# A mixture-of-experts entry on TensorE in another order: all sums of squares behind the first projection, roots on ScalarE, and projections, transposes and router logits ahead of most expert groups

## The reference, cut to what matters

```python
def rms_norm(x):
    eps = jnp.asarray(jnp.finfo(x.dtype).eps, x.dtype)
    return x * jax.lax.rsqrt(jnp.mean(x * x, axis=-1, keepdims=True) + eps)
...
y = jnp.einsum('bhqk,bkhd->bqhd', probs, vr).reshape(bsz, seqlen, dim)
return ternary_linear(rms_norm(y), w_proj)
...
h = h + _L0_attn_ref(_layernorm(h, axis=-1), ...)
h = h + _L0_ffn_ref(_layernorm(h, axis=-1), ...)

def _L0_ffn_ref(hidden_states, gate_w, shared_gate, shared_up, shared_down, r_gate, r_up, r_down):
    x = hidden_states.reshape(-1, h)
    shared_out = _swiglu(x, shared_gate, shared_up, shared_down)
    logits = x @ gate_w.T
    top_id = jnp.argmax(logits, axis=-1)
    score = jax.nn.sigmoid(jnp.max(logits, axis=-1))
    xs = x * score[:, None]
    # routed_out: each token's xs through the SwiGLU of its expert top_id (8 experts)
    return (shared_out + routed_out).reshape(b, s, h)
```

## Time and profile before

| | |
|---|---|
| median of three runs | 574.7 us |
| the profiled execution's own time | 579.41 us |
| its span, first to last instruction | 577.6 us |
| TensorE busy | 419.8 us, 73% |
| VectorE busy | 324.2 us, 56% |
| ScalarE busy | 246.2 us, 43% |
| GpSimd busy | 143.9 us, 25% |
| mean granted TensorE clock | 0.832 |

### The profile page before, as it was taken

How to read it: one execution, slowest core, us unless ns; L and a number is a source line. 1 busy time by engine, 2 the same in 40 slices (tenths; PEclk the granted TensorE clock), 3 DMA queues, 4 the chain that set the end, 5 groups by cost and what they waited for, 6 DMA issues and landing times.

```text
span 577.6 us, 8904 instructions
## 1 busy us (share of the span) xinstructions
PE 419.8 (73%) x3189; PEld 306.6 (53%) x3189; DVE 324.2 (56%) x876; ACT 246.2 (43%) x512; POOL 143.9 (25%) x169
## 2 busy tenths in 40 slices
PE   3677884477779979999889993362497114699997
PEld 3545652256568965666555782221243013489996
DVE  3858875489653410232411116868898995645642
ACT  4235444256634411222212211396099476286661
POOL 3544433089721150000000053800000000213410
PEclk9969887569997997999999998685555555599999
DMA  8921111293003332111101071000000000000002
GB/s 278 406 99 17 20 17 14 82 425 167 2 1 146 111 109 83 36 56 37 49 25 43 23 291 37 0 1 3 1 1 0 1 2 2 1 1 0 1 19 68
DMA packets 19789, 38.59 MB, mean 67 GB/s; under 512 B 2136, under 2 KB 16164, under 8 KB 18340
## 3 DMA queue, kind: packets, MB, share of 16 engines
q1 hardware_dynamic: 18788, 35.41, 17.7%
q0 software_dynamic: 960, 2.62, 1.3%
HBM read 29.77 MB, written 7.01 MB: 64 GB/s over the span
## 4 chain that ended last, share of the span: by engine, by line
PE 46%; DVE 28%; issue 11%; ACT 8%; POOL 5%; DMA 2%; SPq 1%; DVEq 0%; ACTq 0%
PE psum L1253 11%; PE psum L1285 5%; PE psum L2334 4%; PE psum L2367 3%; PE psum L1260 3%; POOL ring L782 2%; PE psum L1299 2%; PE psum L610 2%; PE psum L2373 2%; ACT experts L1662 1%; POOL experts L787 1%; PE psum L921 1%; PE psum L1277 1%; DMA experts<-in_tern 1%; PE psum L2351 1%
## 5 line engine op out<-in xcount | busy, mean ns | idle before, releaser
L1253 PE MATMUL psum<-experts,ring 128*128 x136 | 67.1, 619 | 1.6 <-issue 1.2
L1084 DVE TENSOR_TENSOR ring<-ring,psum 128x512 f32<-128x512 f32 x17 | 11.7, 688 | 67.9 <-PE psum L1253 67.9
L1184 POOL DMA_INDIRECT front<-expert_results,slot_of x10 | 9.5, 953 | 126.4 <-DMA expert_results<-ring 123.7
L1260 PE MATMUL psum<-front,shared 128*128 128x256 f32 (+1 forms) x160 | 36.8, 383 | 0.0
L1253 PEld LDWEIGHTS psum<-experts,ring 128*128 128x128 f32 x136 | 24.4, 199 | 21.0 <-issue 20.9
L1260 PEld LDWEIGHTS psum<-front,shared 128*128 128x128 f32 x160 | 30.3, 197 | 3.5
L1285 PE MATMUL psum<-experts,ring 128*128 x136 | 32.1, 379 | 0.0
L1285 PEld LDWEIGHTS psum<-experts,ring 128*128 128x128 f32 x136 | 25.8, 190 | 10.3 <-issue 7.7
L1382 ACT COPY ring<-psum 128x512 f32<-128x512 f32 x17 | 10.0, 586 | 42.3 <-PE psum L1277 42.3
L2334 PE MATMUL psum<-experts 128*128 128x256 f32 (+1 forms) x120 | 27.4, 371 | 0.0
L590 PE MATMUL psum<-experts,ring 128*128 128x256 f32 x108 | 26.1, 393 | 0.8 <-DVE experts L485 0.7
(11 more groups left out here) (361 smaller groups left out, 1085.7 us busy)
## 6 DMA issues: line engine op xcount, KB each, us to landing
experts<-in_experts SPq DMA_DIRECT2D x8, 1536.0 KB, 12.5
experts<-in_x SPq DMA_DIRECT2D x9, 384.0 KB, 8.3
expert_rows<-zeros SPq DMA_DIRECT2D x1, 2176.0 KB, 14.8
ring<-expert_rows SPq DMA_DIRECT2D x17, 128.0 KB, 2.2
shared<-in_shared SPq DMA_DIRECT2D x1, 1536.0 KB, 18.0
experts<-in_ffn_q SPq DMA_DIRECT2D x1, 1536.0 KB
experts<-in_ffn_s SPq DMA_DIRECT2D x1, 1536.0 KB
experts<-in_pos_embed SPq DMA_DIRECT2D x1, 1152.0 KB, 9.6
```

The lines of the kernel that those rows point to most:

```text
L1084: nc.vector.tensor_tensor(o, o, up_bank(g), ALU.mult).then_inc(hidden_done.sem, 1)
L1253: mm = nc.tensor.matmul(bank, sl_xT[t % 2][:, k, :], slot_w(t, block, k, F), start=(k == 0), stop=(k == KD - 1))
L1260: mm = nc.tensor.matmul(o[:, b, 0:w], shared_w(block, k, (2 * half + b) * P, P), moe_x(c)[:, k, 0:w], start=(k == 0), stop=(k == KD - 1))
```

## The change

```diff
@@ out_scalar
             for c in range(NCH):
                 nc.scalar.activation(out_sq[...], yT[...], ACT.Square).then_inc(y_squared.sem, 1)
+            for part in range(2):
+                act.wait_ge(ms_summed.sem, ms_summed.done(part))
+                r = MS_PARTS[part]
+                nc.scalar.activation(out_ms[:, r[0]:r[-1] + 1], psum[:, 1 + part, 0:len(r)], ACT.Sqrt, bias=out_eps[:, :], scale=1.0 / D).then_inc(ms_ready.sem, 1)
@@ out_tensor
             out_projection(pe, 0)
-            summed(0)
-            summed(1)
+            for t in range(NT):
+                summed(t)
             out_projection(pe, 1)
-            for t in range(2, 6):
-                summed(t)
             out_projection(pe, 2)
-            for t in range(6, NT):
-                summed(t)
-            out_projection(pe, 3)
@@ out_vector
-            def mean(part):
-                dve.wait_ge(ms_summed.sem, ms_summed.done(part))
+            def inverted(part):
+                dve.wait_ge(ms_ready.sem, ms_ready.done(part))
                 r = MS_PARTS[part]
-                nc.vector.tensor_scalar(out_ms[...], psum[...], 1.0 / D, F32_EPS, ALU.mult, ALU.add).then_inc(ms_ready.sem, 1)
+                nc.vector.reciprocal(out_rs[...], out_ms[...]).then_inc(rs_ready.sem, 1)
...
-            joined(0)
-            joined(1)
-            mean(0)
-            for c in range(2, NCH):
+            nc.vector.memset(out_eps[:, :], F32_EPS)
+            for c in range(NCH):
                 joined(c)
+            inverted(0)
             for c in range(NCH):
                 added(c)
-                if c == 0:
-                    mean(1)
-                else:
+                if c >= 1:
                     shifted(c - 1)
                 counted(c)
+                if c == 0:
+                    inverted(1)
             shifted(NCH - 1)
@@ out_pool
-            for part in range(2):
-                pool.wait_ge(ms_ready.sem, ms_ready.done(part))
-                r = MS_PARTS[part]
-                nc.gpsimd.tensor_tensor(out_rs[...], out_ms[...], minus_half[...], ALU.pow).then_inc(rs_ready.sem, 1)
@@ moe_vector
             hidden(0)
+            chosen_experts()
             hidden(1)
-            chosen_experts()
+            routed()
             for g in range(2, GROUPS + 1):
...
-                if g == 2:
-                    routed()
@@ moe_tensor
             turned(0)
+            out_projection(pe, 3)
             logits(0)
+            turned(1)
+            out_projection(pe, NCH - 1)
+            logits(1)
+            turned(2)
             pe.wait_ge(l_shared.sem, l_shared.all)
...
                 if g == 0:
-                    turned(1)
-                    out_projection(pe, NCH - 1)
-                if g == 1:
                     logits(2)
                     turned(3)
-                if g == 2:
-                    logits(4)
                 if g < GROUPS:
                     one_of(g, 1, up_bank(g), up_done)
                 if g == 0:
-                    logits(1)
-                    turned(2)
-                if g == 1:
                     logits(3)
                     turned(4)
+                    logits(4)
+                if g == 1:
+                    rank_tokens()
@@ moe_scalar
             out_normalised(act, 1)
+            columns(1)
+            out_normalised(act, 2)
+            columns(2)
             for g in range(GROUPS + 1):
...
                 if g == 0:
-                    columns(1)
-                    out_normalised(act, 2)
-                    columns(2)
                     out_normalised(act, 3)
-                if g == 1:
                     columns(3)
                     out_normalised(act, 4)
                     columns(4)
+                    score()
+                if g == 1:
+                    scaled(range(0, NT // 2))
                 if g == 2:
-                    score()
-                    scaled(range(0, NT // 2))
-                if g == 3:
                     scaled(range(NT // 2, NT))
```

More of the change, by code:

```diff
@@ L897, in tower @@
         out_shift = sb("out_shift", [P, NT])
+        out_eps = sb("out_eps", [P, 1])
         y_squared, ms_summed, ms_ready, rs_ready = Count("y_squared"), Count("ms_summed"), Count("ms_ready"), Count("rs_ready")
@@ L949, in joined @@
                 nc.vector.tensor_tensor(out_sq[:, 0, w], out_sq[:, 0, w], out_sq[:, 1, w], ALU.add).then_inc(sq_joined.sem, 1)
-            def mean(part):
-                dve.wait_ge(ms_summed.sem, ms_summed.done(part))
+            def inverted(part):
+                dve.wait_ge(ms_ready.sem, ms_ready.done(part))
                 r = MS_PARTS[part]
-                nc.vector.tensor_scalar(out_ms[:, r[0]:r[-1] + 1], psum[:, 1 + part, 0:len(r)], 1.0 / D, F32_EPS, ALU.mult, ALU.add).then_inc(ms_ready.sem, 1)
+                nc.vector.reciprocal(out_rs[:, r[0]:r[-1] + 1], out_ms[:, r[0]:r[-1] + 1]).then_inc(rs_ready.sem, 1)
             def added(c):
@@ L979, in out_vector @@
                 nc.vector.memset(upto[u][:, :, :], 0.0)
-            joined(0)
-            joined(1)
-            mean(0)
-            for c in range(2, NCH):
+            nc.vector.memset(out_eps[:, :], F32_EPS)
+            for c in range(NCH):
                 joined(c)
+            inverted(0)
             for c in range(NCH):
                 added(c)
-                if c == 0:
-                    mean(1)
-                else:
+                if c >= 1:
                     shifted(c - 1)
                 counted(c)
+                if c == 0:
+                    inverted(1)
             shifted(NCH - 1)
         def out_pool(pool):
-            for part in range(2):
-                pool.wait_ge(ms_ready.sem, ms_ready.done(part))
-                r = MS_PARTS[part]
-                nc.gpsimd.tensor_tensor(out_rs[:, r[0]:r[-1] + 1], out_ms[:, r[0]:r[-1] + 1], minus_half[:, 0:len(r)], ALU.pow).then_inc(rs_ready.sem, 1)
             for c in range(NCH):
@@ L1300, in shared_down @@
                                               start=(k == 0), stop=(k == KF - 1))
-                    if c == 0 and u == 0:
-                        rank_tokens()
                 mm.then_inc(sh_down.sem, 1)
```

## The result

The changed kernel took 567.73 us (median of four runs, 566.22 to 569.21) against 575.4 us before (four runs): the ratio is 0.9865, interval 0.9842 to 0.9889, or 7.7 us less (6.4 to 9.1). Forecast were 564.9 us and 9.8 us less, with a range of 562.0 to 570.5; 0.7 us of the difference from 564.9 is that the kernel before took 575.4 here and 574.7 when the forecast was made. The profiled execution took 566.22 us, its span 564.1.

What follows compares the result with a forecast made beforehand. TensorE's own work was taken as the bound: 50.66 us at full clock plus 4.2 of idle made 54.9 instead of 64.66, saving 9.8 us, for a median of 564.9 us; range 562.0 to 570.5.

Steps and rivals of the forecast that it cites:

- rival A: Entry: half clock once, price 3.2 us, saving 6.6, 568.1 us, chance 0.20; twice or ahead of slots, 571.3, chance 0.05.
- the stretch: TensorE from the first projection's start to the end of the slot's first gate and up products, 64.66 us before.
- What bounds the stretch: First projection to first slot products: TensorE's own work bounds it, 50.66 us at full clock; the other 14.00 can move.
- No half clock in the stretch, as no idle is over 1.2: First projection to first slot products: full clock throughout, since 1.59 us of idle had left it full elsewhere.
- the 6.50 us of half clock: Loss behind the entry's idle and the idle ahead of the slots, together 6.50 us, claimed to go.
- The slots' share of the half clock: First slot's gate and up products: 6.52 us where one takes 1.72 at full clock, so 3.08 lost.
- The root on ScalarE: Entry: roots on ScalarE replace GpSimd's powers, 1.65 us for eight columns, at the price of a 1.28 us table load.
- rival C: Entry: a 1.4 us pause behind ScalarE's table load delays both roots; saving 8.4, 566.3 us, chance 0.05.
- Rival D: From 166 to 190 us: thinner work leaves the clock at half throughout; slower, 577.9 us, chance 0.04.
- Rival B: Ahead of the slots: scatters still set their start if `slot_of` is late; 4 us late saves 4.2, 570.5 us, chance 0.06.
- The carry to the end: Behind the first slot products: everything hangs on the slots, so the 9.8 us saving reaches the end whole.

Runs made afterwards that it cites:

- the run with 1.4 us of delay: Changed kernel with five idle VectorE operations ahead of the one that writes `slot_of`; ratio 0.9854 against the kernel before.
- the one with 4.1: Changed kernel with fifteen idle VectorE operations ahead of the one that writes `slot_of`; ratio 0.9972 against the kernel before.
- an order with 2.1 us less idle: Changed kernel with its three entry idles closed by reordering projections, chunk 3's normalisation and chunk 4's transposition; ratio 0.9846 against the kernel before.

## Why the prediction was right, and where not

The time lies in the range, 2.8 us over the forecast and 0.4 under rival A's 568.1. The last is luck: the one of the four executions that was profiled has no half clock in the stretch, so it is the forecast's case and not A's, and A's price turned out wrong.

**What bounds the stretch: right.** The dependencies' idle came as laid out: 1.36, 1.04, 0.67, 0.55 and 0.69 us against 1.2, 1.1, 0.9, 0.55 and 0.45. `moe_top` came 24.7 us behind the first projection (forecast 24.4 from 159.94), `slot_of` 31.5 (30.9). The slots start when TensorE has done group 5 (208.09, without idle), no longer when the scatters are back; the run with 1.4 us of delay shows that the slack is there, the one with 4.1 us what lies behind it.

**"No half clock in the stretch, as no idle is over 1.2": the step that failed.** Of the three profiles of the changed kernel one has full clock throughout; the other two have half clock once in the stretch (from about 163.4 and from about 182.3 us), which is what I had named as the sign that the forecast is wrong. In one TensorE had no idle ahead of it and ran one-column sums; in the other it ran transpositions and eight-column logits between idles of 1.04 and 0.68 us. Over the eight profiles of kernels with ten sums in a row, five have half clock right behind them; of the six with at most five in a row, none. Of the eight with group 0's tail in the changed order, four have it there. These are counts of a few executions: that narrow products matter is likely by them, and why the clock falls in one execution and not in the next stays open.

I had listed both places, under rival A, and given it 0.20 for once and 0.05 for twice, since I read the fall off the length of the idle alone. That reading was incomplete too: the idle of 2.85 us ahead of 348.07, in the same trace, left the granted clock at 1.00, while one of 2.05 did not. A fall cost 0.6 us behind the sums, where an idle follows that absorbs it, and 1.7 behind group 0, not the 3.2 taken from before; in the second profile before, the fall in the entry cost 1.8.

**The size of what goes: over-sized by one profile.** The 64.66 us of the stretch and the 6.50 us of half clock came from one execution. The second has 63.0 us, with 0.8 us less in the first logits and 0.5 less in the first gate product. So 1.0 of the 9.8 goes with the mean before (63.7), and 0.9 after, mostly with the falls (a mean of 55.8 where 54.9 was forecast): 7.9 are left, and the times say 6.9 to 7.7. The slots' share of the half clock, set at 3.08, was 2.8: two products behind an idle take 3.70 us at full clock, and not twice 1.72.

**The root on ScalarE: its price right, its worth nothing.** The load took 1.28 us as in the earlier trace rows. The Trainium skill (ScalarE: Activation LUTs, "What ACT_TABLE_LOAD costs") adds a drain of 1.38 us; here the root starts 0.01 us behind the load, so the trace does not agree with that addition, and rival C falls. But the powers on GpSimd, of which I wrote that they had to go, do no harm once the sums are early: with them the first transposition came 0.46 us sooner.

**Rival D (slower): not so.** Half clock never lasted through the thin stretch; it came back within 4 us each time in the changed kernel's profiles of the stretch. **Rival B:** not in the changed kernel; made to happen with fifteen operations.

**The carry to the end.** I had carried the saving over whole. From the stretch's end to the span's end it is 350.8 us in the second profile before (574.4 - 223.57) and 350.5 in the first one after (564.1 - 213.65), the two that have only 0.72 us of idle ahead of the last `shared_down`: nothing is given back. That is one pair, and no proof for the last microsecond.

## What to carry to other kernels

Where a trace shows one engine busy but for a few idles, add up its idle and what the lower clock costs it between two fixed points: that sum bounds what reordering the same work can bring there. Here it was 14.0 us, 9.8 were forecast from it, and the stretch gained 7.9. Take it from more than one profile, as the cost of the lower clock differed by more than a microsecond between two of the same kernel. And when idle is closed, look at the clock again where narrow products stand together: here an order with 2.1 us less idle had two falls of 1.7 us in its profile and was not clearly faster.

## What the runs showed of the hardware that I had not expected

The granted clock fell to 0.50 with TensorE 100% busy in the trace, behind 2.1 us of one-column products (five of eight profiles). It also fell among transpositions and eight-column logits with an idle of only 0.67 to 0.68 us ahead (at 182 to 186 us in the profile above), where other profiles of the same order kept it full. And in two of the fourteen profiles it fell in the slots, behind an idle of 1.71 us that left it full in the other twelve; this is the changed kernel's second, where products that take 1.98 us elsewhere took 3.57:

```profile
278.88 0.38 PE L1513 MATMUL psum<-identb,qkv_w 128*128 128x128 bf16 x4 [1.71 <-DVE front L1498]
279.68 3.57 PE L1247 MATMUL psum<-experts,ring 128*128 x4 [0.42 <-issue]
```

In twelve of the fourteen profiles, with the first of before among them, TensorE waits 2.9 to 3.6 us ahead of the last `shared_down`, because VectorE's product before it starts late for a reason that the trace calls "remote". In the profile after and in the second of before it waits 0.72. It is in kernels with and without the change. In eleven of the twelve half clock follows, as here in the changed kernel's second profile:

```profile
340.80 5.55 PE L1293 MATMUL psum<-shared,ring 128*128 128x256 f32 x16 [3.56 <-issue]
```

Against 0.72 and 3.87 us that is 4.5 us more. These eleven are all the profiles from the three chips on which the kernel before took 580 us; the other three are from where it took 575. So this one place may hold most of the 5 us by which chips differ. What the wait is for was not followed up.
